# Routed tiles' gated values turned through square moves, down products two tiles behind, unit weights in eight transfers

## What is computed

```python
x = x + 0.5 * ffn(layernorm(x))
x = x + attention(layernorm(x))        # 16 query heads, 4 key heads, rotary
x = x + 0.5 * ffn(layernorm(x))        # the same weights

def ffn(xf):                           # D = 512, F = 352, E = 8, top 2
    y = swiglu(xf, sw1, sw2, sw3)      # shared, 704 wide
    scores = softmax(xf @ gate_w)
    weights, indices = top_k(scores, 2)
    for e in range(8):
        y = y + cw[:, e] * (silu(xf @ rw1[e]) * (xf @ rw3[e])) @ rw2[e]
    return y
```

## Time and profile before

| what | value |
|---|---|
| median of 3 runs | 1610.82 us (1609.36 to 1611.05) |
| the profiled execution, launch to end | 1606.4 us |
| its span, first to last instruction | 1604.6 us |
| mean granted TensorE clock | 0.982 of full |
| TensorE matmul busy | 1543.3 us (96%) |
| VectorE busy | 915.9 us (57%) |
| GpSimd busy | 906.8 us (57%) |
| ScalarE busy | 646.9 us (40%) |
| routed tiles of step 0 | 187.0 to about 431 us |
| routed tiles of step 1 | 1287.6 to about 1532 us |

### The profile page before, as it was taken

How to read it: one execution, slowest core, us unless ns; L and a number is a source line. 1 busy time by engine, 2 the same in 40 slices (tenths; PEclk the granted TensorE clock), 3 DMA queues, 4 the chain that set the end, 5 groups by cost and what they waited for, 6 DMA issues and landing times.

```text
span 1604.6 us, 23987 instructions
## 1 busy us (share of the span) xinstructions
PE 1543.3 (96%) x8100; PEld 1117.0 (70%) x8100; DVE 915.9 (57%) x1558; ACT 646.9 (40%) x968; POOL 906.8 (57%) x753
## 2 busy tenths in 40 slices
PE   8999899999997899999999999999999999999995
PEld 7777799999976774444444444337778889999984
DVE  5553433333378686777777777777554443333335
ACT  4421223333232315666666666663431223233310
POOL 4106196605666857888788788740414368433743
PEclk9999899999998898999999999999999999999997
DMA  9306465525272331112212111023104365444346
GB/s 347 137 7 234 163 206 166 171 86 175 95 231 78 89 74 43 33 34 43 33 33 46 32 34 27 17 64 133 59 1 146 130 240 194 143 141 141 129 131 203
DMA packets 123041, 180.15 MB, mean 112 GB/s; under 512 B 33968, under 2 KB 74800, under 8 KB 120624
## 3 DMA queue, kind: packets, MB, share of 16 engines
q1 hardware_dynamic: 109664, 104.43, 22.1%
q0 software_dynamic: 12832, 73.67, 13.1%
q10 hardware_dynamic: 432, 0.54, 0.1%
HBM read 106.48 MB, written 55.97 MB: 101 GB/s over the span
## 4 chain that ended last, share of the span: by engine, by line
PE 79%; DVE 7%; issue 4%; ACT 3%; POOL 3%; DMA 2%; SPq 2%; another core or an unknown queue 0%; DVEq 0%; POOLq 0%; ACTq 0%
PE PS L1232 11%; PE PS L1233 11%; PE PS L1234 11%; PE PS L1455 7%; PE PS L1469 6%; PE PS L1436 6%; PE PS L1361 3%; PE PS L1364 3%; PE PS L1363 3%; PE PS L1366 3%; PE PS L1362 3%; PE PS L1365 3%; PE PS L1485 3%; PE PS L1376 2%; SPq L1168 1%
## 5 line engine op out<-in xcount | busy, mean ns | idle before, releaser
L1723 ACT ACTIVATE PT<-PS 128x1024 f32<-128x1024 f32 x256 | 258.0, 1024 | 124.0 <-PE PS L1455 119.5
L2036 DVE TENSOR_REDUCE nmf_later<-PS 128x1 f32<-128x1024 f32 x160 | 194.1, 1219 | 59.8 <-PE PS L1436 59.5
L1469 PE MATMUL PS<-PT,V 128*32 128x512 f32 x1024 | 202.9, 605 | 0.0
L2105 POOL TENSOR_TENSOR W<-raw,W 128x544 fp32r<-128x544 f32 x144 | 190.7, 1358 | 1.5
L1455 PE MATMUL PS<-QS,KS 98*128 98x512 f32 x512 | 178.5, 432 | 2.6 <-DVE nmf_later L2036 2.1
L1018 POOL TENSOR_TENSOR added<-PT 128x1024 f32<-128x1024 f32 x56 | 136.4, 2436 | 74.7 <-ACT PT L1723 74.7
L1455 PEld LDWEIGHTS PS<-QS,KS 98*128 98x128 f32 x512 | 85.5, 191 | 127.2 <-issue 50.7
L1436 PE MATMUL PS<-KS,QS 96*128 96x512 f32 x512 | 169.1, 412 | 3.4 <-DVE nmf_first L2036 1.6
L2001 DVE TENSOR_TENSOR thid<-thid,PS 128x352 f32<-128x352 f32 x78 | 40.6, 521 | 196.5 <-ACT thid L1654 196.5
L1232 PE MATMUL PS<-xh,W 128*128 128x512 f32 x352 | 141.5, 402 | 7.4 <-issue 2.7
L1233 PE MATMUL PS<-xl,W 128*128 128x512 f32 x352 | 139.2, 396 | 1.0 <-issue 0.8
(11 more groups left out here) (206 smaller groups left out, 3829.8 us busy)
## 6 DMA issues: line engine op xcount, KB each, us to landing
raw<-ffn_w POOLq DMA_DIRECT2D x18, 2176.0 KB, 10.3
y_routed<-ytile SPq DMA_DIRECT2D x78, 256.0 KB, 2.2
xn<-x_routed SPq DMA_DIRECT2D x160, 64.0 KB, 2.1
x_routed<-xq SPq DMA_DIRECT2D x1, 9984.0 KB, 29.4
xs<-x_routed SPq DMA_DIRECT2D x152, 64.0 KB, 2.1
QS<-later_hi SPq DMA_DIRECT2D x112, 64.0 KB, 2.0
raw<-ffn_w SPq DMA_DIRECT2D x6, 768.0 KB, 6.4
raw<-ffn_w SPq DMA_DIRECT2D x16, 272.0 KB
```

Of the source, the lines that this page charges most:

```text
L1469: e.matmul(PS[i * QUARTER:(i + 1) * QUARTER, ob, :], V[:, b * QT + kt, g, :], PT[:, part_of_unit(u), kt % 2 * GRP:(kt % 2 + 1) * GRP], sta ...
L1723: e.activation(PT[:, part_of_unit(u), :], PS[:, i:i + 2, :].rearrange("p b n -> p (b n)"), ACT.Exp, scale=SCALE).then_inc(p_ready.sem, 1)
L2036: e.tensor_reduce(row_maxima(n)[:, h, t:t + 1], PS[:, i:i + 2, :].rearrange("p b n -> p (b n)"), AX.X, ALU.max, negate=True).then_inc(max_ ...
L2105: low = e.tensor_tensor(W[:, slot, 1, cs], raw[slot][:, cs], W[:, slot, 0, cs], ALU.subtract)
```

## The change

1. **Turning.** The gated values of tile i no longer go to TensorE to be turned. `silu` now writes to a buffer of its own (`shid`), the gate writes `thid`, and four square moves carry `thid` to a new buffer `hsquares`: two are issued by SyncE, two by ScalarE. In item i + 1 VectorE turns all squares at once into the same PSUM bank as before (`turn_hidden`), and `hth` and `htl` are split from it with a reordered view. The rows of `w2` are laid out on the host to fit.
2. **Order.** The down products of tile i now stand behind the up products of tile i + 2. There are two extra items, ("tile", s, 39) and ("tile", s, 40), behind the two halves of the first `LATE` chunk, and `tile_end` stands behind that chunk's gate. In a tile, the 16 products with `xth` come first and the 8 with `xtl` behind them, with a wait of its own for `xtl`.
3. **Weights.** A unit comes in eight transfers of 272 KB. Those of unit 1 are issued at once; those of unit u + 1 between the instructions of the split of unit u: four in the casts, four behind the first four subtractions. What `unit_load` waits for, and where it stands, is as before.
4. **Small things.** The rotary tables are loaded behind the attention weights and no longer at the start. Two routing inputs share a semaphore, and the reloads of two token groups after the attention share one.

```diff
                     work.append(("up", s, step, half))
-                    if g == LATE and k == 0 and half == 0:
-                        work.append(("tile_end", s))
...
+                    if g == LATE and k == 0:
+                        work.append(("tile", s, TILES + half))
...
                 work.append(("gate", s, step))
+                if g == LATE and k == 0:
+                    work.append(("tile_end", s))
...
+    def square_hidden(e, lane, s, i, quadrants):
+        lane.wait_ge(tile_gated, s, i)
+        if i:
+            lane.wait_ge(thid_turned, s, i - 1)
+        for q in quadrants:
+            fs = slice(q * FCH * SQ, min(F, (q + 1) * FCH * SQ))
+            e.dma_start(hsquares[q * SQ:(q + 1) * SQ, :, 0:fs.stop - fs.start],
+                        thid[:, fs]).then_inc(h_in.sem, 16)
...
+                if i >= 3:
+                    tile_store(s, i - 3)
+                if i < TILES:
+                    square_hidden(e, sp, s, i, (0, 1))
...
-            if i:
-                tile_down(s, i - 1)
-            pe.wait_ge(tile_gated, s, i)
-            until_free(BANK_R)
-            for c in range(FCH):
-                rows = f_rows(c)
-                turned = e.transpose(PS[0:rows, BANK_R, c * P:(c + 1) * P], thid[:, c * P:c * P + rows], identf[:])
-            turned.then_inc(thid_turned.sem, 1)
+                if i >= 2:
+                    tile_down(s, i - 2)
...
+                    e.activation(shid[:], PS[:, BANK_A, 0:F], ACT.Silu).then_inc(tile_silu.sem, 1)
...
+                if 1 <= i <= TILES:
+                    act.wait_ge(thid_turned, s, i - 1)
+                    if i >= 2:
+                        act.wait_ge(tile_done, s, i - 2)
+                    e.activation(hth[:].rearrange("p (c i a) -> p c a i", a=P // SQ, i=SQ), hcolumns,
+                                 ACT.Copy).then_inc(thid_hi.sem, 1)
+                if i < TILES:
+                    square_hidden(e, act, s, i, (2, 3))
+                if 2 <= i <= TILES:
+                    tile_out_of_bank(s, i - 2)
...
+        def turn_hidden(s, i):
+            dve.wait_ge(h_in, s, i)
...
+            e.transpose(PS[:, BANK_R, 0:FCH * P],
+                        hsquares[:].rearrange("p a n -> p (a n)")).then_inc(thid_turned.sem, 1)
...
-            e.dma_start(raw[slot][:], ffn_w[u]).then_inc(unit_in[slot].sem, 16)
+            if u == 1:
+                for i in range(SPLITS):
+                    load_piece(u, i)
+
+        def load_piece(u, i):
+            slot, cs = unit_slot(u), split_columns(i)
+            e.dma_start(raw[slot][:, cs], ffn_w[u][:, cs]).then_inc(unit_in[slot].sem, 16)
...
                 pool.step(e.tensor_copy(W[:, slot, 0, cs], raw[slot][:, cs]))
+                if i % 2 and u + 1 < ALL_UNITS:
+                    load_piece(u + 1, i // 2)
...
                 low = e.tensor_tensor(W[:, slot, 1, cs], raw[slot][:, cs], W[:, slot, 0, cs], ALU.subtract)
+                if i < SPLITS // 2 and u + 1 < ALL_UNITS:
+                    load_piece(u + 1, SPLITS // 2 + i)
```

More of the change, by code:

```diff
@@ L327, in shared @@
                 work.append(("gate", s, step))
+                if g == LATE and k == 0:
+                    work.append(("tile_end", s))
+                    work.extend([] if s else [("wqkv_load",)])
+                    ahead = 2 * PAIRS if s else PAIRS
+                    work.extend(gathers[:ahead])
+                    del gathers[:ahead]
                 if g == FIRST[0] and k + 2 < NCH:
@@ L603, in macaron @@
     thid, at = place("thid", (P, F), F32, at)
+    hsquares, at = place("hsquares", (P, P // SQ, FCH * SQ), F32, at)
     hth, at = place("hth", (P, FCH * P), F32R, at)
@@ L635, in macaron @@
     ropeS, _ = place("ropeS", (P, QT, 2, HD), F32, at)
+    shid, _ = place("shid", (P, F), F32, at)
     qka, at = place("qka", (P, 2, NH, HD), F32, x_at + ORDER[0] * TPG * D * 4)
@@ L930, in macaron @@
         elif kind in ("x_early", "x_back"):
-            for g in ORDER[:2] if kind == "x_early" else ORDER[2:]:
+            for g in ORDER[:2] if kind == "x_early" else ORDER[2:3]:
                 x_back[g].plan()
@@ L1064, in tile_load, with tile_store @@
                             ).then_inc(tile_in[i % 2].sem, 16)
+        def tile_store(s, i):
+            sp.wait_ge(y_ready, s, i)
+            e.dma_start(tile_rows(y_routed, i), ytile[:, i % 2, :]).then_inc(tile_out[i % 2].sem, 16)
         for kind, *key in work:
@@ L1119, in sync_program @@
                 tile_load(2)
-            elif kind in ("tile", "tile_end"):
-                s, i = key if kind == "tile" else (key[0], TILES)
+            elif kind == "tile":
+                s, i = key
                 if i + 3 < TILES:
@@ L1996, in vector_program @@
                 tile_columns_lo(s, 0)
+                dve.step(e.memset(hsquares[P - SQ:, :, F - (P - SQ) * FCH:], 0.0))
                 turn_tile(s, 1)
```

123 lines of the change are left out of this document (71 added, 52 removed).

## The result

The changed kernel takes 1648.49 us (median of four runs, 1646.57 to 1649.20), the kernel before 1610.09 in the same comparison: a ratio of 1.0233, with an interval of 1.0214 to 1.0251. The forecast was 1614.7 with a range up to 1630.

| part | before, us | after, us | difference |
|---|---|---|---|
| start to tile 0 of step 0 | 187.0 | 187.9 | +0.9 |
| tile 0 to tile 38, step 0 | 237.9 | 247.6 | +9.7 |
| tile 38 to the last `ytile`, step 0 | 12.0 | 18.4 | +6.4 |
| from there to tile 0 of step 1 | 850.7 | 852.8 | +2.1 |
| tile 0 to tile 38, step 1 | 237.9 | 247.4 | +9.5 |

The account below looks back on a forecast made before the run. TensorE's own instructions were taken to set the pace. Two stretches at -0.9 us, two half-clock losses of 2.5 and 0.7 behind the stretch gave +3.9, so 1610.3; with 4.4 to the median, 1614.7 us, range 1597 to 1630.

Parts of the forecast that it names:

- Turns off TensorE: In each tile, turns and restart cost TensorE 0.34 us; removing them gains 13.3 us a stretch, 9.8 at 0.25.
- The new way of the gated values: Square moves and VectorE's turn between gate and down products: hidden, cost zero as long as moves land within 3.5 us.
- Rival (b): Squares land late behind weight pieces, at 4.5 us: 19 us a stretch, 1653 in all, 1627 at a third; chance 0.13.
- The start: First tiles of a stretch: tile 2 waits for squares under unit 1's load, begins about 199.3; costs 2.7 us.
- Unit 7: Its split on GpSimd stands behind unit 8's load; TensorE waits 8.8 us before its first tile, in both steps.
- (c): GpSimd's issues cost nothing beside its casts: the wait for unit 7 becomes 4.4 us, total 1605.9; chance 0.15.
- (d): Unit 7 is not waited for at all, since the load's wait does not hold the split: 1592 us; chance 0.12.
- The clock behind unit 7: After each 8.8 us wait of TensorE, five us at half clock cost 2.5 us; bounds 0 and 5.
- Rival (a): The clock holds, or the wait is a little shorter: without the 5.0 us, total 1609.7; chance 0.13.
- The end: Behind the tiles: last `ytile` about 439.7, store and gathers 3.3 us later; 0.7 us waiting in step 0, nothing in step 1.
- The sum: Whole kernel: -2 x 0.9 + 2 x 2.5 + 0.7 = +3.9 us against the profiled execution, 1610.3; median forecast 1614.7.

Follow-up runs that it names:

- run with whole units: Changed kernel with each routed or shared unit's weights in one transfer of 2176 KB instead of eight pieces; ratio 1.0662 to the kernel before.
- thin pieces: Changed kernel with each weight piece of units 1 to 9 cut to 32 of 544 columns, 16 KB for 272 KB; ratio 1.0033 to the kernel before.
- order behind the gate: Changed kernel with VectorE's turn of the gated values behind the next tile's gate, using two buffers; ratio 1.0106 to the kernel before.
- pieces alone: Kernel before with only the weights in eight transfers, issued between the casts and subtracts of the unit before; ratio 1.0024, 3.8 us.
- end-alone kernel: Kernel before with only the end of the tiles moved behind the first late chunk's second half and its gate; ratio 1.0073, 11.6 us.
- three moves: Changed kernel with unit 7 split before unit 8's load, turn behind next gate, and tile end behind the first late chunk's first half; ratio 0.9964.
- repeated changed kernel: Changed kernel, unchanged, measured again on another chip; ratio 1.0178 to the kernel before.
- the end sooner: Changed kernel with tiles 39, 40 and `tile_end` all behind the first half of the first late chunk; ratio 1.0227 to the kernel before.
- unit 7 first: Changed kernel with unit 7's split ahead of unit 8's load, whose eight pieces are then issued in one go; ratio 1.0191 to the kernel before.

## Why the prediction was wrong

**Turns off TensorE: right.** Quiet tiles are 5.95 us apart (forecast 5.93), 0.32 us less than 6.27 (forecast 0.34), and that is 13.0 us a stretch (13.3).

**The new way of the gated values: the step that failed first.** It put the cost at nothing "as long as the moves land within 3.5 us", and took zero. The chain itself was right: in a quiet tile (29) the turn of the squares ends 4.3 us behind the gate, forecast 4.7, and an issue of 0.60 us in place of 0.43 did no harm. The condition was wrong. I had let a move behind a piece land "at 3.2 us, just inside"; in the stretch of step 0 the median is 3.1 and the longest 6.0, and 20.0 us went here in both steps (2.5 of them the half clock behind tile 2 of step 1). A move meets more than the rest of one piece, since pieces are issued every 1.7 to 1.9 us and take 4.3 to land. And I took a round robin to mean that a move passes a load nearly unhindered. In the run with whole units the engines did change queues inside the load, and the squares were late by 7 us all the same. The Trainium skill (DMA: Bandwidth & Descriptors, SWDGE vs HWDGE vs iDMA) has the round robin in this section, not in the one that the prediction names. Rival (b) named this mechanism, at 19 us a stretch in full and at a third of that, and had 0.13; it came at half, 10 us a stretch. The thin pieces and the order behind the gate both show it. The row for it was at hand: the 7.0 us of the earlier trace rows stood for loads with slack, and a square has little.

**The start: right in kind, somewhat short.** Tile 2 was put at 199.3, 12.3 us behind tile 0; it came 12.8 us behind it in step 0 and 13.4 in step 1, by waits of 1.30 us at tile 1 and of 3.27 and 3.88 at tile 2, where the forecast had 1.2 and 3. It had no half clock here; in step 1 there was one.

**Unit 7: right in place, cause and size.** 8.8 us forecast, 8.34 and 8.35 measured, ended by GpSimd's subtraction; the split took 19.5 us (376.22 to 395.71; forecast 19.8), a piece's issue 0.55. The pieces alone gave 1.24 us, where the terms of the forecast (3.9 less 2.3 of slack) make 1.6. Rivals (c) and (d) are out.

**The clock behind unit 7: right, a little too dear.** 0.50 behind the gap; 2.0 and 1.5 us, forecast 2.5. Rival (a) is out.

**The end: the second step that failed.** The last `ytile` was well placed: 18.1 us behind tile 38 by the forecast, and 17.8 to its start in the profile. What failed is what follows from it. The prediction said that step 1's "end follows TensorE" and charged 0.7 us in all for moving store, attention weights and gathers, as a wait of a `LATE` silu on ScalarE behind the casts of these weights. I had read TensorE's busy share of the chunks behind the tiles and not the chain through the last store, the gathers, combines and norms: it is two activations of the norm that stand ahead of such a silu, and they cost TensorE 3.8 us and the clock behind. By the end-alone kernel that chain costs 11.6 us; in the changed kernel the two ends are 12.7 us longer, of which the forecast had about 5 as TensorE's own work.

**The sum.** Forecast +3.9, measured +39.9 between the profiled executions. Of the missing 36 us, 20 are the squares, 9 the two ends (12.7 + 2.1, less the 5.7 that the forecast had behind tile 38), and 6 the time ahead of tile 0 and behind the last `ytile` (0.9 + 4.9), which differs by as much between two chips for one kernel.

## What to carry to other kernels

A transfer between buffers that is on an engine's path must be priced by what else is under way when it is issued, at its worst place and not by the median; and what stands behind its wait on the same engine decides what a late one costs. Before a bulk load and a short move share the DMA engines, cut the load into pieces, do not issue them all at once, and put the consumer of the move behind the work that the main engine waits for. Here that order brought the changed kernel from 1.0178 to 1.0233 down to 1.0106; spreading unit 8's pieces on top of the three moves gained nothing that could be measured. When a step's last item is moved, follow the chain from its store to the end of the step, even where the main engine looks busy there.

## What the runs showed of the hardware

- A move of 48 KB between buffers takes 2.0 us to land in the median beside thin pieces of 16 KB, up to 6 or 7 us behind pieces of 272 KB, and 9.4 us behind a transfer of 2176 KB. Its issue takes 0.60 us on SyncE and on ScalarE, where that of 64 KB of a tile's rows takes 0.43.
- Eight pieces of 272 KB issued in 4.25 us hold squares back by nearly as much as a whole unit: they land in 6.4 to 7.3 us.
- DMA engines change between queues inside a transfer of 2176 KB: 46, 47 and 37 records of three queues began in the same 2 us. With eight pieces in one go it looked otherwise: of ScalarE's squares, the first issued at 374.84, no record began before 379.05, while 220 rows of pieces (4352 bytes each) did. What decides the order is not shown.
- Behind gaps of 3.4 to 9.4 us ahead of a tile's products the next interval was 7.3 to 8.8 us in place of 5.95 to 6.05 (0.50 granted in 396:400 of the changed kernel and 254.2:258.2 with whole units); behind gaps of 3.0 to 3.3 us it was so in some cases and not in others; behind one of 2.52 (tile 13 of the repeated changed kernel) it was 6.05. The length of the gap alone does not decide: behind one of only 1.61 (tile 8 with the end sooner) and one of 1.72 (tile 23 of step 1 with unit 7 first) the next interval was 7.60 and 7.58, and 0.50 was granted in 232:234 and 1444:1447.
- The time from the last `ytile` to the last sum on VectorE was 52.8 to 69.6 us in kernels with the same work in it, and for the changed kernel alone 69.6 on one chip and 58.6 on another, with mean granted clocks of 0.81 and 0.88.
